# Cross-attention and a mixture FFN on one core: the normalised tokens made by ScalarE, and sigmoid's last step joined with the mask product

## The reference

```
x = x + xattn(layernorm(x), ctx, ctx)
x = x + ffn(layernorm(x))          # layernorm: (x - mean) / sqrt(var + 1e-5)

ffn(x):                            # 16 heads, head size 64, 8 experts, the best 2 of them
  gate_v = x . Ws ; w, sel = top_k(gate_v, 2)
  mix_v  = one_hot(sel) * sigmoid(w)          # sigmoid of the gate where the expert is chosen, else 0
  v      = mix_v . (x . Wv)
  probs  = softmax(q k^T / 8) ;  attn = probs . v
  mask_o = the 2 best of x . Wd
  return sum over heads and experts of mask_o * attn . Wo
```

## Time and profile before

| | |
|---|---|
| median of 3 runs | 468.41 us (467.52 to 468.84) |
| the profiled execution | 469.56 us, its span 467.7 us |
| busy in the span | PE 412.8 us (88%), DVE 404.1 (86%), ACT 337.7 (72%), POOL 133.6 (29%) |
| mean granted TensorE clock | 0.973 |
| FFN, 212.6 to 440 us (227.4 us) | PE 215.4, DVE 219.1, ACT 173.5, POOL 0 |

### The profile page before, as it was taken

How to read it: one execution, slowest core, us unless ns; L and a number is a source line. 1 busy time by engine, 2 the same in 40 slices (tenths; PEclk the granted TensorE clock), 3 DMA queues, 4 the chain that set the end, 5 groups by cost and what they waited for, 6 DMA issues and landing times.

```text
span 467.7 us, 25765 instructions
## 1 busy us (share of the span) xinstructions
PE 412.8 (88%) x10859; PEld 359.2 (77%) x10859; DVE 404.1 (86%) x775; ACT 337.7 (72%) x924; POOL 133.6 (29%) x142
## 2 busy tenths in 40 slices
PE   1877999999999986578999999999999999999985
PEld 1666789889889875557878788787878878787874
DVE  6897788998989943779999999999999999999962
ACT  6585788788788653366776697688769767876872
POOL 7645788889888650000000000000000000000000
PEclk9999999999999987598999999999999999999999
DMA  7972965465460000000000000000000000000000
GB/s 174 362 239 78 281 208 201 139 204 196 136 202 0 1 4 1 1 1 5 3 7 0 5 5 5 0 5 5 0 5 5 5 0 5 5 2 2 8 8 13
DMA packets 18158, 29.51 MB, mean 63 GB/s; under 512 B 3017, under 2 KB 14025, under 8 KB 18121
## 3 DMA queue, kind: packets, MB, share of 16 engines
q1 hardware_dynamic: 18120, 28.97, 19.5%
HBM read 28.05 MB, written 0.92 MB: 62 GB/s over the span
## 4 chain that ended last, share of the span: by engine, by line
DVE 41%; PE 30%; ACT 13%; issue 12%; DMA 2%; SPq 1%; DVEq 1%; ACTq 0%
DVE ctxf_all L960 9%; DVE ctxf_all L934 6%; PE ps L1062 5%; DVE attnf L971 4%; ACT pf L511 4%; DVE ah L988 4%; PE ps L1296 2%; PE ps L1095 2%; PE ps L1109 2%; ACT e_sb L609 2%; PE ps L1110 2%; PE ps L1111 2%; ACT p L514 2%; PE ps L1077 2%; ACT ctxT L505 2%
## 5 line engine op out<-in xcount | busy, mean ns | idle before, releaser
L609 ACT ACTIVATE e_sb<-ps,smn 128x56 f32<-128x56 f32 x256 | 76.4, 374 | 0.4 <-DVE smn L978 0.4
L609 ACT ACTIVATION_READ_ACCUMULATOR e_sb<-ps,smn 128x1 f32 x256 | 67.2, 274 | 0.0
L960 DVE TENSOR_TENSOR ctxf_all<-mixp,diag_h 128x3584 f16<-128x3584 f16 x32 | 63.2, 2017 | 0.0
L391 POOL TENSOR_TENSOR nat<-ctxf_all,nat 128x640 f16<-128x640 f32 x32 | 55.0, 1719 | 22.8 <-ACT nat L500 22.7
L1062 PE MATMUL ps<-ident,nat 128*128 128x128 f16 x768 | 56.7, 223 | 5.3 <-DVE ctxT L736 2.8
L397 POOL TENSOR_TENSOR p<-pf,p 128x672 f16<-128x672 f32 x32 | 55.3, 1728 | 18.9 <-ACT p L514 18.8
L1062 PEld LDWEIGHTS ps<-ident,nat 128*128 128x128 f16 x768 | 45.0, 99 | 8.1 <-issue 6.5
L500 ACT CAST nat<-ctxf_all 128x1536 f16<-128x1536 f32 x32 | 47.5, 1483 | 4.0 <-DMA ctxf_all<-in_ctx_dram 2.9
L736 DVE COPY ctxT<-ps 128x1024 f16<-128x1024 f16 x64 | 42.3, 681 | 1.7 <-PE ps L1062 1.7
L511 ACT ACTIVATE pf<-ps 128x672 f32<-128x672 f32 x32 | 23.7, 740 | 25.6 <-PE ps L1095 25.6
L1231 PE MATMUL ps<-xn,mT 128*128 128x112 f16 x256 | 41.1, 219 | 0.0
(11 more groups left out here) (172 smaller groups left out, 1235.0 us busy)
## 6 DMA issues: line engine op xcount, KB each, us to landing
ctxf_all<-in_ctx_dram SPq DMA_DIRECT2D x32, 704.0 KB
ctxf_all<-in_ctx_dram SPq DMA_DIRECT2D x32, 46.0 KB
x_all<-in_x_dram SPq DMA_DIRECT2D x4, 224.0 KB
out_dram<-y_all SPq DMA_DIRECT2D x32, 28.0 KB
ctxf_all<-in_ctx_dram SPq DMA_DIRECT2D x32, 18.0 KB
fwq_nat<-in_L_ffn_Wq_dram SPq DMA_DIRECT2D x1, 512.0 KB, 6.2
fwk_nat<-in_L_ffn_Wk_dram SPq DMA_DIRECT2D x1, 512.0 KB, 6.1
fwv_nat<-in_L_ffn_Wv_dram SPq DMA_DIRECT2D x1, 256.0 KB, 5.9
```

The lines of the kernel that those rows point to most:

```text
L391: pool.tensor_tensor(nat[k][:, 1, 7 * C:], ctxf[k][:, 7 * C:], nat[k][:, 0, 7 * C:], ALU.subtract).then_inc(natlo2, 1)
L609: last = act.activation(e_sb[:, k, b, 0:S], ps[:, b, S * k:S * k + S], ACT.Exp, bias=smn[:, K16 * b + k:K16 * b + k + 1], scale=-1.0, accu ...
L960: last = dve.tensor_tensor(dv[:, part, :, :, :], mixp[:, part, :, :].unsqueeze(2).broadcast_to((P, 2 * NQ, HALF, H)), diag_h[:, :, :].unsq ...
```

## The change

`normalise` moves from VectorE to ScalarE. There it is one activation, xn = Identity(x * rstd + shift), whose scale and shift are columns with one number per token; the shift, minus mean times rstd, is made once for all 16 pairs by one new VectorE instruction. On ScalarE it stands right after the second half of `z` and before the copies of the transposed tokens.

The sigmoid is (tanh(g/2) + 1)/2. The instruction that computed it with the factor 4096 goes; the mask product becomes one instruction, (th + 1) * mask, and the factor 2048 moves into TensorE's operand: L1296 now multiplies with `ident_up` = 2048 times the unit matrix, which ScalarE makes once. With `sg` its semaphore goes; ScalarE's `th` now waits for `mix` of the pass before instead of `sg`.

```diff
+        ident_up = sb("ident_up", [P, P])
+        st_shift = sb("st_shift", [P, NP])
-        sg = sb("sg", [P, NQ * HG, E])
...
@@ ScalarE
             act.mul(fwvT[:, :, :], ps[:, 0, :].rearrange("p (e d) -> p e d", e=E), PJ_UP).then_inc(fp_act, 1)
+            act.mul(ident_up[:, :], ident[:, :], 0.5 * MIX_UP)
...
+            def normalise(i):
+
+                act.wait_ge(l2c, 2)
+                after(act, f_xnT, i)
+                act.activation(xn[:, :], x_all[:, bass.ds(i * C, C)], ACT.Identity, bias=st_shift[:, bass.ds(i, 1)],
+                               scale=st_rstd[:, bass.ds(i, 1)]).then_inc(f_xn, 1)
...
                 act.wait_ge(f_ge, i + 1)
-                after(act, f_sg, i)
+                after(act, f_mix, i)
                 act.activation(th[:, :, :], g_sb[:, 0:16, :], ACT.Tanh, scale=0.5).then_inc(f_th, 1)
...
                 if nxt:
+                    normalise(i + 1)
                     xnT_evac(i + 1)
...
             act.wait_ge(c_zero, 21)
+            act.wait_ge(x2c, NP)
+            normalise(0)
             xnT_evac(0)
@@ VectorE
             dve.wait_ge(l2c, 1)
-
-            def normalise(i):
-                after(dve, f_xnT, i)
-                dve.tensor_scalar(xn[:, :], x_all[:, bass.ds(i * C, C)], mv_all[:, bass.ds(i * 2, 1)],
-                                  st_rstd[:, bass.ds(i, 1)], ALU.subtract, ALU.mult).then_inc(f_xn, 1)
+            dve.scalar_tensor_tensor(st_shift[:, :], mv_all[:, :].rearrange("p (n k) -> p n k", k=2)[:, :, 0], -1.0, st_rstd[:, :],
+                                     op0=ALU.mult, op1=ALU.mult).then_inc(l2c, 1)
...
                 after(dve, f_th, i + 1)
-                dve.tensor_scalar(sg[:, :, :], th[:, :, :], 0.5 * MIX_UP, 0.5 * MIX_UP, ALU.mult, ALU.add).then_inc(f_sg, 1)
-                dve.wait_ge(f_sg, i + 1)
                 dve.wait_ge(f_mo, i + 1)
                 after(dve, f_tr, i)
-                dve.tensor_tensor(mix[:, :, :, :].rearrange("p q n e -> p (q n) e"), sg[:, :, :], chosen[:, 0:NQ * HG, :],
-                                  ALU.mult).then_inc(f_mix, 1)
+                dve.scalar_tensor_tensor(mix[:, :, :, :].rearrange("p q n e -> p (q n) e"), th[:, :, :], 1.0, chosen[:, 0:NQ * HG, :],
+                                         op0=ALU.add, op1=ALU.mult).then_inc(f_mix, 1)
...
-                if nxt:
-                    normalise(i + 1)
@@ TensorE
-                            last = pe.matmul(o[:, :, :, first:first + 7:2], ident[:, 32 * h4:32 * h4 + 32],
+                            last = pe.matmul(o[:, :, :, first:first + 7:2], ident_up[:, 32 * h4:32 * h4 + 32],
```

## The result

The changed kernel takes 466.71 us (median of 20 runs), the kernel before 468.63 in the same series: ratio 0.9959, 95% interval 0.9942 to 0.9976, which is 1.9 us less (1.1 to 2.7). The forecast was 2.6 us less, with 465.8 us for the time and 464.2 to 468.3 for the range.

What follows compares the result with a forecast made beforehand. VectorE's work with a detour over TensorE and ScalarE was taken to bound each pass. 0.30 lost less 2.91 gained made -2.61 us: 465.8 us against the median 468.41, range 464.2 to 468.3 for 8 in 10 runs.

Steps and rivals of the forecast that it cites:

- What bounds the kernel: FFN passes of 16.28 us: the chain runs down VectorE, with a detour over TensorE and ScalarE in each pass.
- The detour: From `mix` over TensorE's sums and ScalarE's copy to `mixp`'s low half; ends at 279.42, 0.04 us after VectorE's `pj`.
- `xn`'s slot: VectorE's 0.26 us for `xn` in each pass, beside the detour: removing it gains 0.
- the first rival: Both VectorE slots count, since its own work ends last ahead of `mixp`: another 3.4 us, 462.4 us; chance 0.07.
- `sg` goes: `mix` starts 0.21 us earlier at 12 loop jumps, 0.13 in passes 0, 2 and 15: 2.91 us gained.
- `xn` arrives on ScalarE: Behind the second half of `z` in each pass: an activation of 0.45 us, hidden in 2.04 us of room.
- The start: Ahead of pass 0 nothing covers the column instruction and activation: 0.30 us lost once (0.2 to 0.45).
- the first step: Removal of `sg` in the FFN passes, letting `mix` start earlier: 2.91 us gained.
- The best case: Low end of the whole kernel's forecast from the terms' bounds: 465.1 us, with 3.57 gained and 0.2 lost.
- both slots: In the loop `xn`'s VectorE slot counts too: another 0.26 us in each of 13 passes, 462.4 us; chance 0.07.
- nothing follows: `mix` comes earlier in the passes but half or none of the gain is left: about 468.0 us; chance 0.16.
- no function table is loaded: Denies the rival that ScalarE reloads its table between Identity and exponentials each pass: 15 us slower, about 481; chance 0.02.

Runs made afterwards that it cites:

- each half: Two kernels against the one before: sigmoid joined with the mask product alone, ratio 0.9962; normalised tokens on ScalarE alone, ratio 1.0019.
- the early waits: Changed kernel with two of `mix`'s three waits (`th`, TensorE's sums of the pass before) taken earlier, at the second choice's first instruction: ratio 0.9941.
- the last kernel above: Changed kernel with two waits of `mix` taken earlier, `mix` ahead of the loop's jump, and all normalised tokens kept on VectorE: ratio 0.9955.
- the second half alone: Kernel before with only the normalised tokens moved to ScalarE with the shift column; `sg` and `mix` stay two instructions: ratio 1.0019.

## Why the prediction was right

*What bounds the kernel* held. The detour is 1.38 us in the kernel before, after it, in each half and with the early waits; only VectorE's own list, when it is longer, replaces it. The chain, which names the detour as the later of two ends, was enough to give `xn`'s slot the right price of nothing. That the two ends were only 0.04 us apart made the first rival look closer than it was: an instruction on VectorE that needn't wait starts before its neighbour has ended. In the last kernel above the low half of `mixp` starts 0.60 us behind the start of `pj` (278.10 to 278.70), though `pj` takes 0.68. By that distance VectorE's own list would have let it start at 278.70 + 0.60 = 279.30 in the kernel before, an estimate, where it started at 279.44: the slack was some 0.14 us.

*`sg` goes* had the right mechanism, and its size was somewhat too large. The step was 277.75 + 0.05 + 0.05 = 277.85, hence 0.21 us; measured are 0.17 to 0.18, for the semaphore instruction has a lag of its own on either side (0.05 + 0.05 + 0.04). In passes 0, 2 and 15 the gain is 0.07 to 0.08 us each, where 0.13 was forecast. Summed over these passes and the 12 jumps, the distances from `chosen` to `mix` are 9.07 us before and 6.77 after: 2.29 us gained before rounding, where 2.91 were forecast. The length of the new `mix`, 292 ns, was right. Pass 1 was put at nothing, since TensorE's transposes end last there in the trace before. There the low half of `mixp` follows `mix` by 1.98 us (2.29 with `mix` ahead of the jump and `xn` on ScalarE), but in the six other traces by 1.38 to 1.40: in these pass 1 is like the others, and its 0.08 us counts too.

*`xn` arrives on ScalarE*: hidden, with 2.03 us of waiting behind it. Its length is 0.48 us; the 0.45 from the rows was a little short. The estimate that the Trainium skill gave (ScalarE: Activation LUTs, What ACT_TABLE_LOAD costs) was 0.48 too.

*The start* was mis-sized: 0.30 forecast, 0.44 measured. The column instruction was shorter than taken (0.19), but ScalarE began 0.10 behind it instead of 0.04, ran 0.05 longer, and TensorE began 0.14 behind ScalarE instead of 0.04. The 0.14 could have been read from the kernel before, where TensorE also begins 0.13 behind the end of `xn`. The scaled unit matrix takes ScalarE 0.33 us at 175.9 us, and three copies later ScalarE waits 1.98 us for TensorE, so nothing was the right price for it.

With both terms as measured the sum is 0.44 - 2.29 = -1.85 us, where the forecast had 0.30 - 2.91 = -2.61: 0.62 of the difference is in the first step, 0.14 in the start. The ratio says 1.9 us; its interval, 1.1 to 2.7, holds both sums, so it is the traces and not the ratio that show the forecast as too large. The best case has a slip: its terms, 3.12 and 0.39, are 3.51 us and not 3.57; the 465.1 goes with 3.51.

The rivals: both slots fell with the second half alone. That nothing follows fell with the passes of the changed kernel, which are 0.17 us shorter for a `mix` 0.18 us earlier, and with the early waits, which shorten them again. And no function table is loaded in the loop (five loads in the whole trace, as before).

## What to carry to other kernels

An engine that is busy 96% of a stage can still hold work that costs nothing: look whether the chain leaves it for a detour, and compare the detour with what the engine does meanwhile, from start to start, as neighbours overlap. Taking an instruction away uncovers what stood in its shadow, here a semaphore instruction, so count the waits of the instruction that moves up and put them where long work hides them. And a slot's worth can change with the next edit: when the detour moves, do the comparison again.

## What the runs showed that was not expected

Where the noise sits. The last reciprocal ahead of the FFN, which closes a part that the edits leave alone but for one short activation on ScalarE, starts at 186.10 us in the trace before and 186.38 after, and at 185.19 to 187.90 in the six experiments: 2.7 us between executions.

The first two passes fall into two groups. From `chosen` of pass 0 to that of pass 2 it is 33.92 us before, 33.99 after and 33.86 with `mix` ahead of the jump and `xn` on ScalarE, but 32.34 to 33.04 in the other five traces. What separates the groups is the granted clock from 210 to 215 us. The busy time of that stretch, in the kernel before and in the one with the first pair's tokens on VectorE (columns as in the earlier trace rows):

```profile
210.00:215.00 5.00, 5.00 (x81) 4.59 (x80) 4.11 (x11) 3.20 (x6) 0.00 (x0) 0.66 0.01 3
210.00:215.00 5.00, 4.51 (x148) 4.09 (x149) 4.46 (x9) 3.61 (x6) 0.00 (x0) 1.00 0.01 3
```

The clock is 0.66 in all three traces of the first group, so for a part of the stretch 1.2 GHz, and 1.00 (2.4 GHz) in the five others. From `chosen` of pass 1 to that of pass 2 it is 16.82 to 17.05 us in the three and 15.97 to 16.13 in the five, so some 0.8 us go with it. Why the clock fell is not shown: in the 10 us ahead TensorE was busy for 6.65 to 7.68 us in the three and for 6.67 to 7.75 in the five.

And in the loop's first pass TensorE stops once among the scores without waiting for anything that the profile shows. In the kernel after:

```profile
233.89 1.51 PE L1334 MATMUL ps<-xn1T,xnT 128*32 128x224 f32 x25
236.36 0.58 PE L1334 MATMUL ps<-xn1T,xnT 128*32 128x224 f32 x7 [0.96 <-issue]
```

Before it was 0.40 us, in the experiments 0.25 to 1.03, always behind the 25th of the 32 products; why is open, no run was made for it. With the first pair's tokens on VectorE, a kernel with the same loop as the changed one, it is 0.45, so the change isn't what sets its length.

Each of the three is as large as the change's whole effect or near half of it, so that spans of two single traces don't tell it, while the 11 passes inside the loop repeat to 0.02 us. It can be seen in the two spans, 467.7 and 466.7 us: the trace after reaches the reciprocal 0.28 us later and stops 0.56 us longer among the scores. Without these two the difference of 1.0 us would be 1.8, close to the sum of the terms as measured.
